# Four attention steps' weighted sums in one visit, and VectorE's other work put where it falls due

## The chip, the core and the metric

The kernel runs on one core of a Trainium2 chip. A core has five engines with their own instruction streams: TensorE multiplies matrices and writes PSUM, VectorE and ScalarE work on SBUF and PSUM, GpSimd on SBUF, and SyncE here issues every DMA. Streams run each in its own order and meet at semaphores only. PSUM has eight banks of 128 x 512 float32. The metric is the device time of one execution in microseconds (us).

## What is computed

A layer of attention and MLP, then a layer norm, then a feed-forward block with a choice of one of eight low-rank experts per token, then a layer norm. There are 4 batches of 2048 tokens of width 256, 16 heads of width 16. Only every eighth token attends to all tokens (the others attend to themselves), so a batch has 256 queries.

```python
xn = _ln(x, ln1_g, ln1_b)
q, k, v = split(xn @ w_in.T + b_in)
allowed = (idx % 8 == 0)[:, None] | (idx[:, None] == idx[None, :])
attn = softmax(where(allowed, q k / sqrt(16), -inf))
x1 = x + (attn v) @ w_out.T + b_out
x2 = x1 + gelu(_ln(x1, ln2_g, ln2_b) @ w1.T + b1) @ w2.T + b2
y = layernorm(x + x2)
base = y @ wi_W.T + wi_b
for i in range(8):
    inter = relu(base + (y @ lora_A[i].T) @ lora_B[i].T)
    out += (argmax(y @ gate_W.T + gate_b) == i) * (inter @ wo_W.T + wo_b)
result = layernorm(y + out)
```

## The kernel before

A function, `build_steps`, writes one list of named steps, and every engine walks through this list and issues its own part of each step. So the list sets each engine's order; what a step waits for is a semaphore count that is worked out from the list.

The MLP work is cut into blocks of 512 tokens, M for the first MLP and F for the expert one, and a block into eight items `i` of 128 hidden columns. An item has the steps `up` (two halves: 3 and 3 products of 512 columns, with one more in an F block), `ev` (ScalarE casts the activated item, GpSimd subtracts the cast to get the low part) and `dn` (two halves by tokens, 6 products of 256 columns each). Each float32 factor is split into a high and a low part, so a product is three (`three`, lines 1567 to 1569). `dn` of an item stands two items behind its `up` (`LAG = 2`). When a block's last `dn` has been issued, `sum` adds it to the rows (VectorE, line 1525), `la` takes statistics (lines 1316 to 1330), then `lb` or, for F, `lf` on GpSimd normalises, `st` stores.

To begin a block, `tn` (two parts) turns its rows through the array: four transposes on TensorE (1791), a copy on ScalarE (1179), a subtraction for the low part on VectorE (1512). For an F block `ga` makes the gate logits (16 products, 1803; ScalarE copies them, 1191), `pick` chooses the expert in four parts of three small VectorE operations (1356 to 1373), `pi` turns the choice (1809).

Attention of a batch is 64 steps `s`: head pair `p = s // 8`, key block `kk = s % 8`. A step has `sc` (scores: four products with 50 rows, two head halves side by side, line 1745; ScalarE's exponential into a buffer `prob`, 1172), `mx` (the row maxima of a later pair, 12 steps ahead: two products with 48 rows, 1730; VectorE reduces them, 1442), and `at` (weighted sums: products with 32 columns, line 1756). The last eight maxima of a pair give `ng` (1449 to 1457) and `mt` (a small turn, 1735, that a DMA sends to the scores' operand). After a pair's last step `or` copies the sums out (1466), `ot` turns them (1762), `os` normalises them (1477 to 1482). All `mx` of the attention stages use PSUM banks 2 and 3, `sc` banks 0 and 1, `at` bank 4; `up`, `tn`, `ga`, `pi`, `mt` and `ot` share bank 5, `dn` has 6 and 7. A step that takes a bank waits until its last user's result has been read.

In a stage of attention these steps stand between the MLP items: each item is four quarters (`up` first half, `up` second half, `dn` first half, `dn` second half with `ev`), and 64 steps are spread over the quarters of 16 items (batches 0 and 3) or 24 items (batches 1 and 2). At every even step the two earlier steps' weighted sums come first:

```python
if s % 2 == 0:
    weighted(s - 2)
    weighted(s - 1)
scores(s)
maxima(s)
turns(s)
moves(s)
```

There are two `prob` buffers. `tn`, `ga` and `pi` of the next block hang on the third quarter of set items, `mt` and `ot` (from `turns`) wait in a list and are put in where none of these stands, in the third or last quarter.

Of the kernel before, what the change touches and what calls it, by code (L numbers as in the profile page):

```python
# [44 lines left out]
LEAD = MPP + MPP // 2  # L45
EARLY = LEAD
# [34 lines left out]
def build_steps():  # L81
# [5 lines left out]
    def down(half):  # L87

        if len(pending) <= LAG:
            return  # L90
        i = pending[0]
        put(("dn", i, half))
        if half == 1:
            pending.pop(0)
            if i % FT == FT - 1:
                put(("sum", i // FT))

    def drain():
        while pending:
            i = pending.pop(0)  # L100
            put(("dn", i, 0))
            put(("dn", i, 1))
            if i % FT == FT - 1:
                put(("sum", i // FT))
# [155 lines left out]
    def attention(b):  # L260
# [16 lines left out]
        alone, late = [], []  # L277
# [8 lines left out]
        def turned_out(s, taken):  # L286

            if alone and (alone[0][0][0] == "mt" or len(blocks) == 2 or s % KK in (0, 7) or not taken):
                for one in alone.pop(0):
                    put(one)  # L290
                    if one[0] == "ot":
                        late.append(("os", *one[1:]))
# [3 lines left out]
        def moves(s):  # L296
            p, kk = s // KK, s % KK
            if kk == 1 and p and p + 2 < PAIRS:
                put(("kld", b, p + 2))
            if s == 4:  # L300
# [10 lines left out]
        def step(s):  # L311

            if s % 2 == 0:
                weighted(s - 2)
                weighted(s - 1)
            scores(s)
            maxima(s)
            turns(s)
            moves(s)

            while late:
                put(late.pop(0))

        s, hook = 1, []

        places = [(0, 2, 4, 7)] * 2 if len(blocks) == 2 else [(0, 2, 3, 7), (0, 1, 3, 7), (1, 2, 4, 7)]
        for quarter in range(4 * n):

            ahead = min(2, quarter // 2) if len(blocks) == 2 else 0
            while s < STEPS_B and s * 4 * n <= (quarter + ahead) * STEPS_B:  # L330
                step(s)
                s += 1
            i, part = FT * blocks[0] + quarter // 4, quarter % 4
            k, f = i // FT, i % FT
            ready = k + 1
            at = places[k - blocks[0]]
            if part == 0:
                put(("up", i, 0))
            elif part == 1:
                put(("up", i, 1))  # L340
                pending.append(i)
                after(k - 1, f, 4)
                rows_in(k, f, 6)
                if f == at[2] + 1:
                    put(("pick", ready, 1))
                if f == at[2] + 2:
                    put(("pick", ready, 3))
            elif part == 2:
                down(0)
                hook = dict(zip(at, ([("tn", ready, 0)], [("tn", ready, 1), ("xw", ready)], [("ga", ready)], [("pi", ready)]))).get(f, [])  # L350
                taken = bool(hook)
                if hook and hook[0][0] == "pi" and alone and alone[0][0][0] == "mt":
                    turned_out(s, False)
                for one in hook:
                    put(one)
                if not hook:
                    taken = turned_out(s, False)
            else:
                put(("ev", i))
                turned_out(s, taken)  # L360
                down(1)
                if f == at[2]:
                    put(("pick", ready, 0))
                if f == at[2] + 1:
                    put(("pick", ready, 2))
        assert s == STEPS_B and not alone and not late
# [3 lines left out]
    def tail(b):  # L370
# [32 lines left out]
        while pending:  # L403
            i = pending.pop(0)
            put(("dn", i, 0))
            put(("dn", i, 1))
# [37 lines left out]
def N(*step):  # L444
    return COUNT[step]

# [41 lines left out]
for _s in STEPS:  # L488
# [26 lines left out]
    elif _w == "dn" and _s[1] % FT == 0:  # L515
# [86 lines left out]
def attention_ffn_kernel(nc, x, w_in, b_in, w_out, b_out, w1, b1, w2, b2, ln1_g, ln1_b, ln2_g, ln2_b,  # L602
                         gate_W, gate_b, wi_W, wi_b, wo_W, wo_b, lora_A, lora_B, out):
    ctx = ExitStack()
    with ctx:
# [74 lines left out]
        prob = [place(f"prob{i}", [P, 2, 2, QW], F32, m0 + 4096 * i)[0] for i in range(2)]  # L680
# [12 lines left out]
        x1g, _ = place("x1g", [P, NQ, D], F32, r1 + 5120)  # L693

# [99 lines left out]
        def _(sp):  # L794
# [25 lines left out]
            def step(what, *a):  # L820
# [75 lines left out]
                elif what == "ldg":  # L896
                    sp.wait_ge(stq, 48 * KT * N("pq", b))
# [71 lines left out]
        def _(pool):  # L969
# [10 lines left out]
            def step(what, *a):  # L980
# [6 lines left out]
                elif what == "xc":  # L987
                    c = a[1]
                    n = N("xc", b, c)
                    x_c = xin[PLACE[c] % XB]  # L990
                    if n > 4:
# [872 lines left out]
```

## Time and profile before

| | |
|---|---|
| median of 3 runs | 1442.04 us (1440.31 to 1442.88) |
| the profiled execution's span, first to last instruction | 1437.3 us |
| TensorE busy in the span | 1386.3 us (96%), 10103 products |
| VectorE, ScalarE, GpSimd busy | 854.4, 734.6, 647.8 us |
| granted TensorE clock, mean | 0.995 |
| attention stages in the span, about | 159 to 312, 480 to 655, 823.5 to 998, 1167 to 1320 us |

The profile is of one execution; for it only its span is known, which lies 4.7 us under the median of the timed runs. A product is shown with the time from its start to its modelled end, while the next one starts earlier; so the busy share overstates, and the distances from start to start tell the pace. In brackets stands the idle time of the engine before an instruction and what released it.

### The profile page before, as it was taken

Reading aid. Unit: us, or ns where it says so; the run is one execution under the profiler, and the core shown is the slowest. Engines: PE = TensorE matmul, PEld = TensorE weight load, DVE = VectorE, ACT = ScalarE, POOL = GpSimd, SP = SyncE. Lnnn points to the kernel's source line nnn. Section 1 sums busy time; section 2 is a strip of 40 time slices with the busy share of each in tenths; the row PEclk is TensorE's granted clock in tenths of the full one; section 3 lists DMA queues with packets and bytes.
Section 4 is the critical chain, followed back from the end, with each engine's and each line's share of the span. In section 5 each row is a group of like instructions: output and inputs, shape, how many; then the busy total and the mean of one; then the engine's idle time right before and its main releaser. Section 6 shows DMA issues by size and latency. Waiting matters only on the chain.

```text
span 1437.3 us, 26412 instructions
## 1 busy us (share of the span) xinstructions
PE 1386.3 (96%) x10103; PEld 1066.3 (74%) x10103; DVE 854.4 (59%) x1823; ACT 734.6 (51%) x1103; POOL 647.8 (45%) x533
## 2 busy tenths in 40 slices
PE   6799999999999999999999999999999999999997
PEld 5688665678888766668888866667888876556996
DVE  6748576636656666555647576763675657762332
ACT  3444555553544555564444555555444455655442
POOL 3554321328754414145865432333776442132755
PEclk9899999999999999999999999999999999999999
DMA  7565223215561132212682213220556212310100
GB/s 246 161 181 107 57 45 67 55 38 192 190 164 47 50 68 51 56 45 84 210 214 62 74 38 75 57 53 20 189 189 158 74 45 44 80 26 23 52 16 30
DMA packets 91394, 130.51 MB, mean 91 GB/s; under 512 B 8314, under 2 KB 68180, under 8 KB 88148
## 3 DMA queue, kind: packets, MB, share of 16 engines
q1 hardware_dynamic: 91268, 128.82, 32.9%
q8 instruction: 81, 1.33, 0.4%
q14 instruction: 45, 0.37, 0.1%
HBM read 68.08 MB, written 60.57 MB: 90 GB/s over the span
## 4 chain that ended last, share of the span: by engine, by line
PE 79%; DVE 10%; POOL 4%; issue 2%; ACT 2%; DMA 0%; SPq 0%; POOLq 0%; DVEq 0%; ACTq 0%
PE ps L1567 19%; PE ps L1568 16%; PE ps L1569 16%; PE ps L1756 8%; PE ps L1745 7%; PE ps L1730 4%; DVE mx L1442 3%; PE ps L1803 2%; PE ps L1791 2%; PE ps L1825 2%; DVE stats L1316 2%; POOL rows L1042 1%; ACT prob L1172 1%; PE ps L1688 1%; PE ps L1762 1%
## 5 line engine op out<-in xcount | busy, mean ns | idle before, releaser
L1442 DVE TENSOR_REDUCE mx<-ps 128x2 f32<-128x1024 f32 x256 | 311.1, 1223 | 179.0 <-PE ps L1730 176.9
L1172 ACT ACTIVATE prob<-ps 128x1024 f32<-128x1024 f32 x256 | 262.6, 1026 | 180.4 <-PE ps L1745 180.2
L1057 POOL TENSOR_TENSOR hid1l<-gel,hid1h 128x512 fp32r<-128x512 f32 x85 | 111.2, 1309 | 202.2 <-ACT hid1h L1214 202.1
L1057 POOL TENSOR_TENSOR hid2l<-gel,hid2h 128x512 fp32r<-128x512 f32 x85 | 111.1, 1307 | 197.6 <-ACT hid2h L1214 197.5
L1057 POOL TENSOR_TENSOR hid0l<-gel,hid0h 128x512 fp32r<-128x512 f32 x86 | 112.4, 1307 | 191.6 <-ACT hid0h L1214 191.5
L1206 ACT ACTIVATE gel<-ps,cols 128x512 f32<-128x512 f32 x128 | 88.2, 689 | 180.7 <-PE ps L1569 169.5
L1745 PEld LDWEIGHTS ps<-qslot,kslot 50*128 50x128 f32 x1024 | 76.2, 184 | 91.0 <-issue 65.8
L1208 ACT ACTIVATE gel<-ps 128x512 f32<-128x512 f32 x128 | 76.6, 598 | 120.9 <-PE ps L1825 119.7
L1756 PE MATMUL ps<-prob,vals 128*32 128x256 f32 x2048 | 137.5, 385 | 0.2
L1745 PE MATMUL ps<-qslot,kslot 50*128 50x256 f32 x1024 | 128.9, 330 | 4.2 <-ACT prob L1172 4.1
L1730 PE MATMUL ps<-kslot,qslot 48*128 48x512 f32 x512 | 105.8, 424 | 4.8 <-DVE mx L1442 4.4
L1756 PEld LDWEIGHTS ps<-prob,vals 128*32 128x32 f32 x2048 | 53.2, 109 | 54.9 <-ACT prob L1172 14.8
L1036 POOL TENSOR_TENSOR rstd<-vare,mhalf 128x4 f32<-128x4 f32 x47 | 48.3, 1028 | 76.6 <-DVE vare L1330 74.9
L1042 POOL TENSOR_SCALAR rows<-rows,mv,rstd 128x256 f32<-128x256 f32 x60 | 73.5, 1234 | 0.0
L1567 PE MATMUL ps<-turned0h,wih 128*128 128x512 f32 x128 | 58.8, 459 | 0.0
L1730 PEld LDWEIGHTS ps<-kslot,qslot 48*128 48x128 f32 x512 | 46.3, 184 | 16.5 <-DVE mx L1442 8.8
L1567 PE MATMUL ps<-turned1h,wih 128*128 128x512 f32 x128 | 57.2, 447 | 0.0
L1214 ACT ACTIVATE hid0h<-gel 128x512 fp32r<-128x512 f32 x86 | 54.0, 628 | 1.3
L1567 PE MATMUL ps<-turned1h,w1h 128*128 128x512 f32 x128 | 54.3, 424 | 0.1
L1512 DVE TENSOR_TENSOR turned1l<-ps,turned1h 128x512 fp32r<-128x512 f32 x32 | 22.1, 690 | 54.3 <-ACT turned1h L1179 54.2
L1214 ACT ACTIVATE hid2h<-gel 128x512 fp32r<-128x512 f32 x85 | 53.5, 629 | 1.3
L1214 ACT ACTIVATE hid1h<-gel 128x512 fp32r<-128x512 f32 x85 | 53.4, 628 | 1.3
(245 smaller groups left out, 3943.9 us busy)
## 6 DMA issues: line engine op xcount, KB each, us to landing
k_d<-kst SPq DMA_DIRECT2D x192, 128.0 KB
kslot<-k_d SPq DMA_DIRECT2D x64, 384.0 KB
xin<-in_L_attn_x SPq DMA_DIRECT2D x32, 256.0 KB, 4.3
rows<-xs_d SPq DMA_DIRECT2D x16, 512.0 KB, 6.3
y_d<-rows SPq DMA_DIRECT2D x15, 512.0 KB, 3.1
rows<-y_d SPq DMA_DIRECT2D x15, 512.0 KB, 4.5
out<-rows SPq DMA_DIRECT2D x15, 512.0 KB, 3.2
xs_d<-xin SPq DMA_DIRECT2D x28, 256.0 KB, 2.7
```

The source lines that it names most:

```text
L1042: nc.gpsimd.tensor_scalar(y[:, i, :], y[:, i, :], mv[:, k % 2, i, 0:1], rstd[:, k % 2, i:i + 1], ALU.subtract, ALU.mult).then_inc(final_do ...
L1057: nc.gpsimd.tensor_tensor(hid[i % RING][1][:], gel[i % 2][:], hid[i % RING][0][:], ALU.subtract).then_inc(lo_done, 1)
L1172: nc.scalar.activation(prob[(n - 1) % 2][:].rearrange("p e i q -> p (e i q)"), ps[:, 0:2, :].rearrange("p a n -> p (a n)"), ACT.Exp).then_ ...
L1206: nc.scalar.activation(gel[i % 2][:], ps[:, UP, :], ACT.Gelu, bias=cols[:, B1C + f:B1C + f + 1]).then_inc(act_done, 1)
L1214: nc.scalar.activation(hid[i % RING][0][:], gel[i % 2][:], ACT.Copy).then_inc(hi_done, 1)
L1442: nc.vector.tensor_reduce(best[:, :, j % NQ], ps[:, at:at + 2, :], AX.X, ALU.max).then_inc(maxr_done, 1)
L1567: mm(o, l[0], r[0], start=start, stop=False, skip_group_check=True)
L1568: mm(o, l[0], r[1], start=False, stop=False, skip_group_check=True)
L1569: return mm(o, l[1], r[0], start=False, stop=stop, skip_group_check=True)
L1730: last = mm(ps[:, bank + e, :], qslot[p % SLOTS][half, P * t:P * t + P], kslot[p % SLOTS][half, 512 * piece:512 * piece + 512], start=True ...
L1745: last = mm(ps[:, e, QW * i:QW * i + QW], kslot[p % SLOTS][half, at:at + P], qslot[p % SLOTS][half, :], start=True, stop=True)
L1756: last = mm(ps[at:at + PR, OUT, 0:QW], vals[:, v:v + PR], prob[(n - 1) % 2][:, e, i, :], start=kk == 0, stop=kk == KK - 1)
```

## The change

A visit takes one step, and every fourth visit two: the scores and maxima of step s, then the weighted sums of four steps (s - 3 to s), then scores and maxima of s + 1. A stage is cut into three parts an item (16 items) or four (24 items, a visit at every second part), so that 48 visits lie evenly. `prob` has four buffers; the two new ones lie over `xg` and `x1o`, which is why the residual load `ldg` moves to the last step and some waits are added. `dn` is issued in four parts instead of two, `sum` in two halves, each with its half of the statistics (`ls`) behind it, and `la` right after. The four `pick` parts stand right behind `ga`. Only `os` is kept back, to the visit behind.

```diff
+GROUP = 4
...
+        def job(cost, *what):
+            if what[0][0] == "os":
+                jobs.append((cost, unit[0], what))
+            else:
+                for one in what:
+                    put(one)
...
+        def visit(s):
+
+            unit[0] += 1
+            taken = [s]
             scores(s)
             maxima(s)
-            turns(s)
-            moves(s)
...
+            if s % GROUP == GROUP - 1 or s == STEPS_B - 2:
+                slot(1.25)
+                for one in range(s + 1 - GROUP, s + 1) if s % GROUP == GROUP - 1 else (s - 2, s - 1):
+                    weighted(one)
+                scores(s + 1)
+                maxima(s + 1)
+                taken.append(s + 1)
+            for one in taken:
+                turns(one)
+                moves(one)
+            slot(small)
+            return taken[-1] + 1
+
+        def down_part(i, h, j):
+            put(("dn", i, h, j))
+            if i % FT == FT - 1 and j == 1:
+                blk = i // FT
+                job(0.7, ("sum", blk, h))
+                job(0.8, ("ls", blk, 2 * h), ("ls", blk, 2 * h + 1))
+                if h == 1:
+                    job(0.8, ("la", blk))
...
+        parts = 3 if len(blocks) == 2 else 4
...
+            if s < STEPS_B and (parts == 3 or at_part % 2 == 0):
+                s = visit(s)
...
+                if hook and hook[0][0] == "ga":
+                    for what in range(4):
+                        job((1.4, 0.6, 0.8, 0.6)[what], ("pick", ready, what))
...
-        prob = [place(f"prob{i}", [P, 2, 2, QW], F32, m0 + 4096 * i)[0] for i in range(2)]
...
+        prob = [place(f"prob{i}", [P, 2, 2, QW], F32, at)[0] for i, at in enumerate((m0, m0 + 4096, r1 + 3072, r1 + 8192))]
```

TensorE in the first items of batch 0's attention, before. `qslot` by `kslot` are scores, `kslot` by `qslot` maxima, `prob` by `vals` weighted sums, `ust` the end of an `up`.

```order
L1825 MATMUL ps<-ust,bst 128x512
L1756 MATMUL ps<-prob_107,vals 32x256 x4
L1756 MATMUL ps<-prob_108,vals 32x256 x4
L1745 MATMUL ps<-qslot_115,kslot_112 128x256 x4
L1730 MATMUL ps<-kslot_113,qslot_116 128x512 x2
```

The same place now:

```order
L1921 MATMUL ps<-ust,bst 128x512
L1841 MATMUL ps<-qslot_113,kslot_110 128x256 x4
L1826 MATMUL ps<-kslot_111,qslot_114 128x512 x2
L1852 MATMUL ps<-prob_120,vals 32x256 x4
L1852 MATMUL ps<-prob_121,vals 32x256 x4
L1852 MATMUL ps<-prob_122,vals 32x256 x4
L1852 MATMUL ps<-prob_123,vals 32x256 x4
L1841 MATMUL ps<-qslot_113,kslot_110 128x256 x4
L1826 MATMUL ps<-kslot_112,qslot_115 128x512 x2
```

Sums of four steps now stand in one row, between two pairs of scores and maxima.

TensorE a few products later in the same item, before. `ident,rows` are the four transposes of `tn`, `ident,negs` is the small turn `mt`.

```order
L1569 MATMUL ps<-w2h,hid1l 128x256
L1791 MATMUL ps<-ident,rows_97 128x128 x4
L1756 MATMUL ps<-prob_107,vals 32x256 x4
L1756 MATMUL ps<-prob_108,vals 32x256 x4
L1745 MATMUL ps<-qslot_115,kslot_112 128x256 x4
L1730 MATMUL ps<-kslot_114,qslot_117 128x512 x2
L1735 MATMUL ps<-ident,negs 8x128
L1567 MATMUL ps<-w2h,hid1h 128x256
```

The same place now:

```order
L1665 MATMUL ps<-w2h,hid1l 128x256
L1887 MATMUL ps<-ident,rows_97 128x128 x4
L1831 MATMUL ps<-ident,negs 8x128
L1663 MATMUL ps<-w2h,hid1h 128x256
L1664 MATMUL ps<-w2l,hid1h 128x256
```

The small turn follows the transposes at once; a visit stood between.

VectorE behind the second gate of batch 0's attention stage, before. `mx<-ps` are the maxima's reductions, `uall`, `pickm` and `picke` the choice.

```order
L1356 TENSOR_TENSOR uall<-gcopy 128x160
L1357 TENSOR_TENSOR uall<-uall,gateb 128x4x8
L1358 TENSOR_REDUCE pickm<-uall 128x4
L1442 TENSOR_REDUCE mx<-ps 128x2 x2
L1360 TENSOR_TENSOR picke<-uall,pickm 128x32
L1361 TENSOR_TENSOR picke<-picke,rank 128x32
L1362 TENSOR_REDUCE pickm<-picke 128x4
L1466 COPY oraw<-ps 128x256
L1442 TENSOR_REDUCE mx<-ps 128x2 x2
```

The same place now, from the second operation of the choice:

```order
L1449 TENSOR_TENSOR uall<-uall,gateb 128x4x8
L1450 TENSOR_REDUCE pickm<-uall 128x4
L1452 TENSOR_TENSOR picke<-uall,pickm 128x32
L1453 TENSOR_TENSOR picke<-picke,rank 128x32
L1454 TENSOR_REDUCE pickm<-picke 128x4
L1456 TENSOR_TENSOR picke<-picke,pickm 128x32
L1458 TENSOR_TENSOR uall<-uall,picke 128x4x32
L1461 CAST us<-uall 128x4x32
L1463 TENSOR_TENSOR us<-uall,us 128x4x32
L1464 COPY us<-us 128x4x32
L1465 MEMSET us 128x4x2
L1534 TENSOR_REDUCE mx<-ps 128x2 x3
```

All twelve operations of a choice now stand between two reductions.

## Rows read from the trace of the kernel before

**Rows 1.** The profile page's head: span and instructions.

```profile
span 1437.3 us, 26412 instructions
```

**Rows 2.** By stage: us, busy of TensorE, its loads, VectorE, ScalarE, GpSimd; clock.

```profile
159.00:312.00 153.00, 148.56 (x1265) 91.87 (x1264) 95.11 (x175) 92.24 (x122) 36.65 (x29) 1.00 0.23 51
480.00:655.00 175.00, 172.78 (x1445) 116.23 (x1444) 105.32 (x200) 103.75 (x142) 54.96 (x43) 1.00 0.22 52
```

**Rows 3.** Timeline (start, length, engine, line), TensorE: a visit without sums.

```profile
823.26 0.28 PE L1569 MATMUL ps<-w2h,hid0l 128*128 128x256 f32 x1
823.47 0.51 PE L1745 MATMUL ps<-qslot,kslot 50*128 50x256 f32 x4
823.81 0.40 PE L1730 MATMUL ps<-kslot,qslot 48*128 48x512 f32 x2
...
824.37 0.28 PE L1568 MATMUL ps<-w2l,hid0h 128*128 128x256 f32 x1
```

**Rows 4.** Timeline, TensorE: a visit with two steps' sums.

```profile
844.22 0.28 PE L1569 MATMUL ps<-wfh,hid0l 128*128 128x256 f32 x1
844.43 1.07 PE L1756 MATMUL ps<-prob,vals 128*32 128x256 f32 x16
845.43 0.51 PE L1745 MATMUL ps<-qslot,kslot 50*128 50x256 f32 x4
...
846.44 0.40 PE L1568 MATMUL ps<-turned0l,wih 128*128 128x512 f32 x1
```

**Rows 5.** Timeline, TensorE: sums straight behind maxima.

```profile
171.21 0.50 PE L1730 MATMUL ps<-kslot,qslot 48*128 48x512 f32 x2
171.64 1.39 PE L1756 MATMUL ps<-prob,vals 128*32 128x256 f32 x16
```

**Rows 6.** Costliest groups: busy, mean ns, idle before and releaser; the maxima.

```profile
L1730 PE MATMUL ps<-kslot,qslot 48*128 48x512 f32 x512 | 105.8, 424 | 4.8 <-DVE mx L1442 4.4
```

**Rows 7.** Timeline, TensorE: scores that wait for an exponential.

```profile
1305.70 0.50 PE L1745 MATMUL ps<-qslot,kslot 50*128 50x256 f32 x4
1307.32 0.50 PE L1745 MATMUL ps<-qslot,kslot 50*128 50x256 f32 x4 [0.23 <-ACT prob L1172]
```

**Rows 8.** Timeline, all engines: maxima that wait for a reduction.

```profile
559.71 1.23 DVE L1442 TENSOR_REDUCE mx<-ps 128x2 f32<-128x1024 f32 x1
...
560.99 0.50 PE L1730 MATMUL ps<-kslot,qslot 48*128 48x512 f32 x2 [0.22 <-DVE mx L1442]
...
561.53 1.23 DVE L1442 TENSOR_REDUCE mx<-ps 128x2 f32<-128x1024 f32 x1 [0.60 <-PE ps L1730]
```

**Rows 9.** Timeline, VectorE: operations of a choice.

```profile
570.06 1.25 DVE L1357 TENSOR_TENSOR uall<-uall,gateb 128x32 f32<-128x32 f32 x1
...
644.82 0.18 DVE L1364 TENSOR_TENSOR picke<-picke,pickm 128x32 f32<-128x32 f32 x1
...
645.96 0.23 DVE L1372 COPY us<-us 128x128 f32<-128x128 f32 x1
```

**Rows 10.** Timeline, VectorE: sum and statistics of a finished block.

```profile
554.72 1.27 DVE L1525 TENSOR_TENSOR rows<-rows,ps 128x512 f32<-128x512 f32 x2
...
557.78 1.40 DVE L1316 BATCH_NORM_STATS2 stats<-rows 128x6 f32<-128x256 f32 x4
```

**Rows 11.** Timeline, all engines: transposes, their low part, the small turn.

```profile
188.32 0.60 PE L1791 MATMUL ps<-ident,rows 128*128 128x128 f32 x4
...
189.65 0.68 DVE L1512 TENSOR_TENSOR turned0l<-ps,turned0h 128x512 fp32r<-128x512 f32 x1
...
190.39 0.28 PE L1735 MATMUL ps<-ident,negs 128*8 128x128 f32 x1
```

**Rows 12.** Timeline, TensorE: a turn behind gate products, transposes behind a turn.

```profile
815.10 0.27 PE L1735 MATMUL ps<-ident,negs 128*8 128x128 f32 x1 [0.53 <-ACT gcopy L1191]
...
537.72 0.64 PE L1809 MATMUL ps<-ident,us 128*98 128x128 f32 x4 [0.36 <-ACT mT L1153]
```

**Rows 13.** Timeline, ScalarE: the first exponential of a stage.

```profile
824.91 1.02 ACT L1172 ACTIVATE prob<-ps 128x1024 f32<-128x1024 f32 x1
```

More of the change, by code:

```diff
@@ L91, in down @@
         i = pending[0]
-        put(("dn", i, half))
+        for j in range(2):
+            put(("dn", i, half, j))
         if half == 1:
@@ L95, in down @@
             if i % FT == FT - 1:
[L96 to L104, printed above, removed]
+                for h in range(2):
+                    put(("sum", i // FT, h))
     def piece(b, q, part):
@@ L275, in weighted, with slot, flush @@
                     put(("or", b, s // KK))
-        alone, late = [], []
+        alone, jobs, unit = [], [], [0]
+        def job(cost, *what):
[4 more added lines that the diff above has]
+                    put(one)
+        def slot(room):
+            spent = 0.0
+            while jobs and jobs[0][1] < unit[0] and (not spent or spent + jobs[0][0] <= room):
+                cost, _, what = jobs.pop(0)
+                spent += cost
+                for one in what:
+                    put(one)
+        def flush(*kinds):
+            while any(one[0] in kinds for _, _, what in jobs for one in what):
+                for one in jobs.pop(0)[2]:
+                    put(one)
         def turns(s):
@@ L286, in turned_out @@
         def turned_out(s, taken):
-            if alone and (alone[0][0][0] == "mt" or len(blocks) == 2 or s % KK in (0, 7) or not taken):
+            if alone and (alone[0][0][0] == "mt" or len(blocks) == 2 or s % KK in (0, 5, 6, 7) or not taken):
+                if alone[0][0][0] == "ot":
+                    flush("os")
                 for one in alone.pop(0):
@@ L309, in moves @@
                         put(one)
[L311 to L315, printed above, removed]
+        small = 0.5 if len(blocks) == 2 else 1.0
+        def visit(s):
+            unit[0] += 1
+            taken = [s]
             scores(s)
             maxima(s)
-            turns(s)
-            moves(s)
-            while late:
-                put(late.pop(0))
-        s, hook = 1, []
-        places = [(0, 2, 4, 7)] * 2 if len(blocks) == 2 else [(0, 2, 3, 7), (0, 1, 3, 7), (1, 2, 4, 7)]
@@ L327, in attention @@
[L327 to L333, printed above, removed]
+            if s % GROUP == GROUP - 1 or s == STEPS_B - 2:
[5 more added lines that the diff above has]
+                taken.append(s + 1)
@@ new lines, in ended @@
+        def ended(k, f):
+            if k < 0:
+                return
+            what = BLOCKS[k][0]
+            if what == "M" and f == 4:
+                flush("la")
+                put(("lb", k))
+            if what == "F" and f in (3, 4):
+                flush("la")
+                put(("lf", k, f - 3))
+            if f == 5:
+                put(("st", k))
+        s = 1
+        places = [(0, 2, 4, 7)] * 2 if len(blocks) == 2 else [(0, 2, 3, 7), (0, 1, 3, 7), (1, 2, 4, 7)]
+        parts = 3 if len(blocks) == 2 else 4
@@ L334, in attention @@
+        owed = None
+        for at_part in range(parts * n):
+            if s < STEPS_B and (parts == 3 or at_part % 2 == 0):
+                s = visit(s)
+            i, part = FT * blocks[0] + at_part // parts, at_part % parts
             k, f = i // FT, i % FT
@@ L404, in tail @@
             i = pending.pop(0)
-            put(("dn", i, 0))
-            put(("dn", i, 1))
+            for h in range(2):
+                for j in range(2):
+                    put(("dn", i, h, j))
         for h in range(2):
@@ L1314, in ln_a @@
                 j = k % 2
[L1315 removed]
+                for i in range(CT if ("ls", LN_STEPS[k][1], 0) not in COUNT or LN_STEPS[k][0] != "la" else 0):
                     nc.vector.bn_stats(stats[:, j, i, :], y[:, i, :]).then_inc(stat_done, 1)
```

114 lines of the change are left out of this document (74 added, 40 removed).

## The prediction, made before the changed kernel ran

> **What bounds the kernel now.** I read the span first, then the busy time by stage, then TensorE's starts inside one stage. The span is 1437.3 us [rows 1]; the median of the three timed runs, 1442.04, is 4.7 above it, so I add a change of the span to the median. Only the four attention stages change their order. Two are short (batches 0 and 3: two MLP blocks of eight items beside 64 steps), two are long (batches 1 and 2: three blocks). One of each is shown: TensorE is busy 148.6 of 153 us and 172.8 of 175 at a granted clock of 1.00, its 2.4 GHz level, VectorE 95 and 105, ScalarE 92 and 104 [rows 2]. So TensorE's order sets the time, and another engine counts only where TensorE stands and waits for it. Busy hides part of such waits, since a product is shown for 0.28 to 0.5 us while the next can start after 0.11 to 0.23. I therefore go by starts.
>
> **What an attention visit costs.** A visit with scores and maxima alone: last down product 823.26, second one after the visit 824.37, 1.11 us; two down products at their free pace of 0.12 taken off leave 0.87 [rows 3]. A visit with two steps' weighted sums ahead: 844.22 to 846.44, 2.22, less one down (0.12) and one up product (0.23), leaves 1.87; from the first sum's product to the scores it is 1.00 for 16 products, that is 0.216 for each four, and the rest is the turn between the array's tilings [rows 4]. From maxima to weighted sums there are only two cases, 0.43 from start to start [rows 5], of which 0.21 is the maxima's own work.
>
> **What the change saves.** Four steps were two visits of each kind, 2 x 0.87 + 2 x 1.87 = 5.48. Now they are two single visits and one group: entry 0.21, scores to maxima 0.34, maxima to sums 0.43, eight rounds of four 1.87 to the next scores, 0.34, then 0.65 until the second product behind; 3.84 less 0.35 for two ordinary products is 3.48. With the singles 5.22: 0.26 saved for each visit that goes. The order has 62 to 64 visits in a stage before and 48 now, so 14 and 16 go: 2 x (14 + 16) x 0.26 = **-15.7 us**.
>
> Second, TensorE's waits of before go or move. Its idle before maxima products, mostly for VectorE's reduction, is 4.8 us in all [rows 6]; with the hidden part, and with those before scores and before small transposes, taken as every start in these stages that is over 0.04 us later than is usual for its pair, I find 10 us in a short stage and 4 in a long one: **-28 us** at most, if all go. The exponentials' part does go: in the group three sums stand ahead of the one that needs the newest exponential, and the single visits lie 1.8 us apart or more, where scores that wait for an exponential start 1.62 after the scores ahead [rows 7].
>
> **What the change adds.** All maxima of these stages share one pair of PSUM banks. A reduction ends, the next maxima product follows 0.05 later (559.71 + 1.23, 560.99), and its reduction starts 0.54 after it [rows 8], which I take as 0.45 where the product had not waited. So two maxima products need some 1.72 us. In a short stage the single visits now follow one another 1.9 and 1.8 us apart, in a long one 2.3 and 2.5, and 2.63 lie between a group's two. Whatever VectorE does between two reductions beyond the gap that these leave (0.6 to 0.7, 1.1 to 1.3, 1.4) delays the later one, and TensorE stands at the maxima after that.
>
> Gate choice. The twelve small operations of a gate stood in four quarters, several reductions apart; now all stand between two reductions. Free, the last six take 1.4 us from 644.82 on, the first six as much. An operation that meets GpSimd's subtraction takes 1.25 (570.06), where those six average under 0.25 [rows 9], and ScalarE's copy that releases that subtraction now follows the gate's copy at once, so I take one meeting: 4.0 us, bounds 2.9 and 5. In a long stage, from a maxima product as zero: six down products to 1.14, sixteen gate products to 2.73, the gate's copy done 0.8 later, choice from 3.55 to 7.55, the next reduction from there to 8.8. The maxima product behind it would have started at 6.5: 2.3 us of waiting. In a short stage, 3.3. Two gates of a long stage and one of a short one have maxima behind them: 4 x 2.3 + 2 x 3.3 = **+15.8**.
>
> Here the page named SBUF — State Buffer of the Trainium skill (Who interferes with whom) bears: an operation of VectorE with two SBUF inputs and a GpSimd instruction that reads SBUF take turns whole, by who starts first. The 1.25 us agree. By it the meeting costs at most one subtraction, and the sum is the above; had the two engines shared without waiting, it would be 6 us less.
>
> Block ends. Sum and statistics of a finished block, 1.27 us and, from 557.78 to the reduction at 559.71, 1.93 [rows 8, 10], were one visit or more apart; now half of them follow the first down half, the other half the second, with one reduction at most between. In a long stage nothing is between: 3.4 us where 1.1 are free and the next maxima have 0.8 to spare, 1.45; with a turned block's low part (0.68) in the same place twice, 1.7 and 1.85. In a short stage 0.5 + 1.3, and with the output normalisation in it 2.3. 2 x (5.0 + 4.1) = **+18.2**.
>
> The shared bank. Transposes, gate products and up products use one PSUM bank. Before, a turned block's transposes and the small turn of the maxima had a visit between; in the short stages the two now stand back to back, four times in each. The turn must wait until ScalarE has copied and VectorE has subtracted: transposes from 188.32 on, the last at 188.65, subtraction 189.65 to 190.33, turn at 190.39 [rows 11]. That is 1.7 after the last transpose, where 0.11 is the free pace: 8 x 1.6 = **+12.7**. A turn right behind gate products idles 0.53, and four transposes right behind a turn 0.36 [rows 12]; 0.17 more is hidden in each. New are two of the first kind without maxima behind (0.7) and ten of the second, the turned output behind the turn (0.5): **+6.6**.
>
> The start. The first scores now have the second ones 1.56 us behind them in each stage. The first exponential starts at 824.91 for scores at 823.47 and takes 1.02 [rows 3, 13], so the second scores wait 0.96: 4 x 0.96 = **+3.8**. Product starts after a wait lose about 0.1 more, some 24 times, and small things (copies ahead of exponentials, the last visits without maxima) 0.4 to 1 a stage: **+4**.
>
> At nothing I cost: the down step cut in halves (same products, one wait less), the key loads a step earlier (they wait for the same scores as before), two more buffers for the exponentials, and the residual load put at the stage's end. That load, two GpSimd additions of 1.3 us and the subtraction behind them come before the down products of that item, which stand two items later; if that cover failed it would cost up to 3 us a batch.
>
> **Sum.** -15.7 - 28 + 15.8 + 18.2 + 12.7 + 6.6 + 3.8 + 4 = **+17.4 us**: span 1454.7, median **1459**. Bounds of the unknown: choice without the meeting -6, with two +6; halves of the block end better hidden -5; the output normalisation meeting the subtraction in short stages (1.7 instead of 0.76) up to +10; the turn from maxima to sums, from two cases, -3 to +3. Together some 1448 to 1472.
>
> **Rivals.** *VectorE keeps pace* (faster): the merged visits bring 15.7 and the old waits 28, and the bursts land where TensorE has other work. It decides at the maxima product two visits after a burst: if that starts on time, picks, block ends and most bank waits are not paid, and between 20 and 40 us of new waits are left: 1442 - 44 + 20 = 1418, up to 1438. For it speaks that VectorE is busy only 60% of the stages; against it, that one bank pair serves all maxima. Chance 0.18. *A wash*: a quarter to a third of the added terms is hidden, 1438 to 1445, chance 0.12. *The bursts pile up* (slower than I say): a late reduction pushes the next burst into the next gap, and the projection behind starts with a delayed GpSimd: 1473 to 1485, chance 0.08. *The order does not do what is said*: the instruction order shows four steps' sums between two scores, so I give it nothing.
>
> [...]
>
> **How the numbers follow.** Forecast, 1446 to 1472: 0.62. A comparison of this kernel can tell about 0.2%, 2.9 us. Faster by more takes the first rival and a little of the wash: 0.2; the same: 0.1; slower: 0.7. The range leaves out the quicker half of the first rival and the piled-up case: 1430 to 1473.
>
> **What would show it.** Right: maxima products idle for VectorE's reduction by 25 us or more in all (4.8 now); idle before the small turn and the turned output for ScalarE and VectorE, over 10 us; stages of about 156 and 181 us. Wrong: long stages under 172 us, choice bursts after which the next maxima start on time, or a projection that changes by over 1 us.

## The result: 36 us slower, twice the forecast

The changed kernel takes 1476.85 us (median of six, 1476.07 to 1483.98), the kernel before 1441.17: 35.7 us more, a ratio of 1.026 (95% interval 1.0244 to 1.0280). Forecast were 17.4 us more, 1459, and a range up to 1473. The direction was right and the size was not. Where one execution of a version lay far above its others (6478 us in e10_turns_apart, 1551 in e7_long_waits), it is left out of that version's median below.

The profiled execution is the slowest of the six. The head of its page, and its row for the maxima (that of before is in [rows 6]):

```profile
span 1482.2 us, 26416 instructions
L1826 PE MATMUL ps<-kslot,qslot 48*128 48x512 f32 x512 | 105.8, 424 | 34.7 <-DVE mx L1534 32.3
```

The idle time before maxima has gone from 4.8 to 34.7 us. By stage (the columns of [rows 2]: us, busy of TensorE, its loads, VectorE, ScalarE, GpSimd, granted clock, DMA), the four attention stages, and the first projection between them:

```profile
163.00:327.00 164.00, 146.51 (x1264) 94.71 (x1263) 97.12 (x175) 92.24 (x122) 34.95 (x27) 0.97 0.21 48
327.00:496.00 169.00, 167.20 (x1067) 146.14 (x1059) 104.58 (x239) 75.32 (x128) 108.40 (x90) 1.00 0.46 134
496.00:678.00 182.00, 170.73 (x1444) 120.24 (x1443) 106.41 (x200) 102.73 (x142) 54.30 (x42) 0.98 0.22 50
847.30:1029.40 182.10, 170.84 (x1445) 120.44 (x1443) 106.39 (x200) 102.84 (x142) 54.26 (x42) 0.98 0.21 50
1198.30:1364.60 166.30, 148.72 (x1260) 95.32 (x1259) 93.63 (x162) 91.77 (x121) 33.44 (x25) 0.95 0.20 42
```

From first scores to last sums the stages were 152.6, 174.7, 174.7 and 152.5 us; they are 164.0, 181.9, 182.0 and 166.3: 39.9 more in all. The long ones are 1 us above the forecast (181), the short ones 8 to 10 above it (156). The projection is the same to 1 us. Another 4 us of this execution lie ahead of the first stage, in code that the change leaves alone; the other executions have spans of 1474 to 1476.

The column to look at is the last but two: the granted clock was 1.00 in every attention stage before, and it is 0.95 to 0.98 now.

**One burst, close up.** First VectorE and TensorE together in the second stage (start, length, engine, line): the gate choice, the maxima behind it, the products behind those.

```profile
526.81 0.33 DVE L1448 TENSOR_TENSOR uall<-gcopy 128x160 f32<-128x160 f32 x1 [1.86 <-ACT gcopy L1283]
...
527.35 0.39 PE L1826 MATMUL ps<-kslot,qslot 48*128 48x512 f32 x2
...
527.62 1.11 DVE L1452 TENSOR_TENSOR picke<-uall,pickm 128x32 f32<-128x32 f32 x1
527.68 1.93 PE L1852 MATMUL ps<-prob,vals 128*32 128x256 f32 x32
...
529.54 0.50 PE L1841 MATMUL ps<-qslot,kslot 50*128 50x256 f32 x4
...
530.64 0.07 DVE L1465 MEMSET us<- 128x8 f32 x1
530.74 1.23 DVE L1534 TENSOR_REDUCE mx<-ps 128x2 f32<-128x1024 f32 x1
...
532.02 0.57 PE L1826 MATMUL ps<-kslot,qslot 48*128 48x512 f32 x2 [1.98 <-DVE mx L1534]
...
532.53 0.79 PE L1663 MATMUL ps<-turned0h,wih 128*128 128x512 f32 x1
...
533.12 0.63 PE L1664 MATMUL ps<-turned0l,wih 128*128 128x512 f32 x1
533.55 0.63 PE L1665 MATMUL ps<-turned0h,wil 128*128 128x512 f32 x1
```

The maxima of 527.35 are done before 527.8, but their reduction has to wait behind the whole choice (526.81 to 530.71, with one operation that met GpSimd, 1.11 us) and starts at 530.74. The next maxima, ready behind the scores of 529.54, start at 532.02. That much was foretold: a choice of 4.0 us and a wait of 2.3. What was not: the up products behind the wait start 0.59 and 0.43 apart, where 0.34 and 0.23 are usual. The same place by stretches:

```profile
529.00:532.30 3.30, 1.32 (x18) 0.61 (x10) 2.96 (x10) 1.02 (x1) 0.00 (x0) 1.00 0.00 0
532.30:535.70 3.40, 3.40 (x9) 2.15 (x7) 2.76 (x7) 0.00 (x0) 0.00 (x0) 0.50 0.00 0
535.70:539.00 3.30, 2.94 (x24) 2.19 (x23) 1.23 (x1) 2.59 (x5) 0.56 (x1) 1.00 0.02 5
```

TensorE stood for most of the first stretch; in the second it is busy throughout at a granted clock of 0.50, its 1.2 GHz level, while its products start further apart; in the third the clock is back. Eleven such places lie in the four stages (one is twice as long, and the expectation of e1_all_due counts it as two), none in those of before. By the stage rows the loss is at most 164.0 x 0.03 + 182 x 0.02 x 2 + 166.3 x 0.05 = 20.5 us. Taking every product that starts in one of these stretches and how much later it comes than is usual behind its neighbour, I find **17.8 us**. I call this the clock's loss below, and give it for each kernel's profiled execution.

What TensorE waited for in the stages (us in total, times, longest):

```profile
PE ps L1826 <- DVE mx L1534: 32.3, 26, 2.3
PE ps L1831 <- DVE turned1l L1604: 5.7, 4, 1.4
PE ps L1831 <- DVE turned0l L1604: 5.7, 4, 1.4
PE ps L1831 <- ACT gcopy L1283: 3.7, 7, 0.5
PE ps L1858 <- ACT mT L1237: 3.6, 10, 0.4
PE ps L1841 <- ACT prob L1264: 3.6, 4, 0.9
```

These are the waits of the prediction, but for 8 of the 26 before maxima (the copy, taken apart below) and two more small turns behind gate products than it had. The largest part of what was missing looked like the clock. That, and the terms themselves, is what the experiments test.

### The profile page after: what moved, and what is told of

It reads as the page before. It is cut to its first block, busy times and chain, and to the rows that moved or that the text cites. A ratio compares the mean times of both kernels' runs of the same rounds, so it can differ in the third digit from the quotient of the medians.

```text
span 1482.2 us, 26416 instructions
## 1 busy us (share of the span) xinstructions
PE 1385.8 (93%) x10103; PEld 1084.2 (73%) x10103; DVE 863.6 (58%) x1823; ACT 732.4 (49%) x1103; POOL 647.8 (44%) x533
## 4 chain that ended last, share of the span: by engine, by line
PE 75%; DVE 12%; POOL 4%; issue 3%; ACT 2%; DMA 0%; SPq 0%; POOLq 0%; DVEq 0%; ACTq 0%
PE ps L1663 18%; PE ps L1664 15%; PE ps L1665 15%; PE ps L1852 8%; PE ps L1841 6%; PE ps L1826 4%; DVE mx L1534 3%; PE ps L1899 2%; PE ps L1921 2%; PE ps L1887 2%; POOL rows L1126 1%; DVE stats L1408 1%; ACT prob L1264 1%; DVE rows L1616 1%; PE ps L1858 1%
## 5 line engine op out<-in xcount | busy, mean ns | idle before, releaser
L1826 PE MATMUL ps<-kslot,qslot 48*128 48x512 f32 x512 | 105.8, 424 | 34.7 <-DVE mx L1534 32.3
L1852 PE MATMUL ps<-prob,vals 128*32 128x256 f32 x2048 | 130.5, 396 | 0.0
L1852 PEld LDWEIGHTS ps<-prob,vals 128*32 128x32 f32 x2048 | 61.1, 113 | 51.7 <-issue 18.9
L1558 DVE COPY oraw<-ps 128x256 f32<-128x256 f32 x32 | 13.6, 425 | 80.2 <-PE ps L1852 50.8
L1137 POOL TENSOR_TENSOR rows<-rows,wob 128x1024 f32<-128x1024 f32 x16 | 38.1, 2380 | 43.0 <-PE ps L1887 43.0
L1663 PE MATMUL ps<-wfh,hid0h 128*128 128x256 f32 x176 | 55.6, 316 | 0.0
```

The costliest lines, as they stand in the source:

```text
L1663: mm(o, l[0], r[0], start=start, stop=False, skip_group_check=True)
L1826: last = mm(ps[:, bank + e, :], qslot[p % SLOTS][half, P * t:P * t + P], kslot[p % SLOTS][half, 512 * piece:512 * piece + 512], start=True ...
L1852: last = mm(ps[at:at + PR, OUT, 0:QW], vals[:, v:v + PR], prob[prob_of(p, kk)][:, e, i, :], start=kk == 0, stop=kk == KK - 1)
```

## The experiments

Line numbers differ a little between the versions; the names in the rows are the same. For each kernel:

| version | us | ratio to before (95%) | idle before maxima | clock's loss |
|---|---|---|---|---|
| changed kernel | 1476.85 | 1.026 (1.0244 to 1.0280) | 34.7 | 17.8 |
| e4_fill | 1466.84 | 1.019 (1.0178 to 1.0208) | 16.7 | 4.6 |
| e2_pick_due | 1457.49 | 1.013 (1.0112 to 1.0142) | 22.0 | 11.8 |
| e3_ends_due | 1460.39 | 1.014 (1.0129 to 1.0159) | 18.2 | 14.3 |
| e1_all_due | 1439.20 | 1.0005 (0.999 to 1.002) | 7.9 | 0 |
| e5_turn_first | 1468.51 | 1.020 (1.0175 to 1.0222) | 23.7 | 22.3 |
| e10_turns_apart | 1468.31 | 1.021 (1.0179 to 1.0247) | 36.4 | 25.9 |
| e6_due_and_apart | 1434.18 | 0.996 (0.9944 to 0.9977) | 1.4 | 10.6 |
| e9_all_apart | 1427.55 | 0.9915 (0.9901 to 0.9929) | 8.5 | 0 |
| e11_sum_at_once | 1419.00 | 0.985 (0.9839 to 0.9864) | 9.3 | 1.6 |
| e12_copy_later | 1410.44 | 0.979 (0.9774 to 0.9811) | 1.8 | 0 |
| e7_long_waits (kernel before, delayed) | 1480.51 | 1.029 (1.0269 to 1.0320) | 32.3 | 13.9 |
| e8_short_waits (kernel before, delayed) | 1480.18 | 1.028 (1.0264 to 1.0299) | 29.3 | 3.1 |

**Is it the clock?** Some 220 products whose results nobody reads go into 22 of the long waits; they write an unused half of a PSUM bank.

```diff
+FILL = {(b, m // MPP, m % MPP): n for b in range(B) for m, n in
+        (((23, 6), (34, 14), (55, 12)) if b in (0, LAST) else ((19, 7), (24, 13), (40, 9), (46, 14)))}
...
+if what == "mx":
...
+    fill(FILL.get(a, 0))
+elif what == "mt" and seen[1] == "tn":
+    fill(9)
```

> The changed kernel with extra products, whose results nobody reads, put on TensorE into 22 of its long waits (the 14 longest ones before maxima, 6 to 14 products each, and the 8 before the small turn behind transposes, 9 each); nothing else moves, every wait ends when it did. Theory A: the granted clock stays at 1.00 in the stages and the time falls although work was added, by up to the 17.8 us that the half-clock stretches hold: 1463 us (1459 to 1468). Theory C (the low clock is a mark of idle time and costs nothing; the 18 us that the prediction lacks are waits): 1475 us or more.

1466.84 us: 10 us faster with more work. The place shown above, here in TensorE's timeline (L1776 is the filler):

```profile
522.92 0.50 PE L1861 MATMUL ps<-qslot,kslot 50*128 50x256 f32 x4
523.26 1.70 PE L1776 MATMUL ps<-kslot,qslot 48*128 48x256 f32 x13
525.37 0.50 PE L1846 MATMUL ps<-kslot,qslot 48*128 48x512 f32 x2 [0.41 <-DVE mx L1534]
525.80 0.50 PE L1663 MATMUL ps<-turned0h,wih 128*128 128x512 f32 x1
526.14 0.39 PE L1664 MATMUL ps<-turned0l,wih 128*128 128x512 f32 x1
526.37 0.39 PE L1665 MATMUL ps<-turned0h,wil 128*128 128x512 f32 x1
```

The maxima start 2.45 us after the scores (525.37 less 522.92); without filler it was 2.48. The wait is as long as ever, yet the up products behind it are 0.34 and 0.23 apart again. The stages by the same view:

```profile
160.70:320.10 159.40, 150.77 (x1332) 101.02 (x1331) 97.09 (x175) 92.14 (x122) 35.11 (x27) 1.00 0.22 49
489.30:669.80 180.50, 174.41 (x1488) 124.56 (x1486) 106.33 (x200) 102.83 (x142) 54.02 (x42) 0.99 0.22 51
838.60:1017.50 178.90, 172.79 (x1487) 123.21 (x1486) 106.34 (x200) 102.78 (x142) 54.22 (x42) 1.00 0.22 51
1186.50:1348.80 162.30, 153.61 (x1329) 101.88 (x1327) 93.57 (x162) 91.89 (x121) 32.35 (x25) 0.98 0.20 43
```

The clock's loss falls by 13.2 us (17.8 to 4.6), the four stages of the profiled executions by 13.3 (694.4 to 681.1), the median of all executions by 10. In all 22 places TensorE still idles 0.15 to 0.58 us between the last filler product and the one that waits, so no wait got longer. Theory C, that low clock is a mark and not a cost, is out.

**Long waits or idle time as such?** Two kernels without anything of the change, only the kernel before with reductions repeated in the long stages: three reductions five times, or 24 twice. The first as an edit (the second does it once more, at every second index from 14 to 60):

```diff
+for again in range(4 if b in (1, 2) and MPP * p + j in (28, 40, 52) else 0):
+    nc.vector.tensor_reduce(best[:, :, j % NQ], ps[:, at:at + 2, :], AX.X, ALU.max).then_inc(again_done, 1)
...
```

> The kernel before, with nothing of the change: in each long stage three reductions are done five times instead of once, so that the next maxima wait some 4.3 us, six times in all, 26 us of waits. Theory A (each wait this long is followed by a stretch at half clock that costs 1.7 us or more): 26 + 10, so 1476 us (1471 to 1482), six stretches. Theory C (a wait costs its length): 1466 (1462 to 1469), whatever the clock reads.

> The kernel before, with 24 reductions of each long stage done twice: by the spacing of the maxima there, waits of 0 to 0.8 us, 21 us in all, none long. Theory A: no stretch at half clock, 1461 us (1456 to 1467), the waits alone. If it is the sum of idle time and not the single long wait after which the clock falls, stretches at half clock show here too and the time is 1470 or more.

The long waits: 1480.51 us (three executions, 1480.24 to 1485.06), inside the range of theory A; six waits of 4.4 to 5.5 from start to start, and a stretch at half clock behind each of the six. By starts, the long stages got 27.7 us more of waits and 13.9 of clock's loss. One of the six, its maxima and the two stretches on both sides of it:

```profile
532.91 0.80 PE L1735 MATMUL ps<-kslot,qslot 48*128 48x512 f32 x2 [4.59 <-DVE mx L1447]
...
528.00:532.00 4.00, 0.32 (x4) 0.11 (x2) 3.90 (x4) 1.43 (x2) 0.00 (x0) 0.97 0.63 109
532.00:538.50 6.50, 5.59 (x32) 3.27 (x32) 2.08 (x2) 0.44 (x2) 0.00 (x0) 0.50 0.00 0
```

The short waits missed their expectation: 1480.18 against 1461. The extra reductions met VectorE's other work oftener than the spacing of the maxima had told, and the waits came to 33.7 us, not 21. For the clock the run is clear all the same. More waiting, by 48 repeated reductions and mostly in short pieces, has a clock's loss of only 3.1: two stretches, each right behind one of the few long waits (2.45 and 1.73 us late; two others, of 2.10 and 1.76, had none). Here the long waits cost half of themselves again (13.9 of 27.7), the time in small pieces a tenth (3.1 of 33.7). That the waits of the maxima alone, without groups of four steps, bring the clock down is shown too.

**The bursts.** The changed kernel has a waiting list from which VectorE's work could come out piece by piece at later visits, but lets only the output normalisation into it. These three let in more:

```diff
-if what[0][0] == "os":
+if what[0][0] in ("os", "pick", "sum", "ls", "la"):
```

> The changed kernel, but VectorE's gate choice (four parts) and the sum and statistics of a finished block stand in the waiting list and come out one by one at later visits, where the changed kernel puts them down at once; TensorE's order stays. Theory A (bunched work of VectorE makes the maxima wait, and each wait of some 2 us is followed by a stretch at half clock): TensorE's idle before maxima falls from 32 us to about 10, the transposes' 8 waits of 1.7 stay, stretches at half clock go from 12 to 4 or fewer, time 1443 us (1435 to 1452). Theory B (the merged visits leave too little room between the maxima, whoever stands between them): waits of 25 us or more stay and the time is above 1465.

> The changed kernel with only the gate choice handed out over later visits; block ends stay bunched. By the prediction's term the choices cost 15.8 us of waits; with their share of the half-clock stretches (theory A) 22 to 25, so 1453 us (1447 to 1462). If the choices are harmless, 1474 or more.

 (here only "pick" is added)

> The changed kernel with only sum and statistics of finished blocks handed out over later visits; choices stay bunched. By the prediction's term block ends cost 18.2 us; with the half-clock stretches behind them about 23, so 1454 us (1448 to 1464). If they are harmless, 1474 or more.

 (here "sum", "ls" and "la")

1439.2, 1457.5 and 1460.4 us. With choice and block ends handed out, the 36 us are gone: TensorE's order of the changed kernel, VectorE's work spread, and the time is that of before. The choices alone bring 19.4 (6.0 of it the clock's loss, by the profiled executions), the block ends alone 16.5 (3.5). The maxima's row in the first of them, and its long stage:

```profile
L1826 PE MATMUL ps<-kslot,qslot 48*128 48x512 f32 x512 | 102.5, 410 | 7.9 <-DVE mx L1534 7.5
...
479.70:651.60 171.90, 167.15 (x1445) 117.84 (x1443) 102.19 (x200) 102.83 (x142) 53.99 (x42) 1.00 0.23 53
```

Theory B, that merged visits leave too little room whoever stands between them, falls. The ten executions of this version spread from 1433.8 to 1443.8, those above 1441.5 all at a mean granted clock of 0.989, the 1433.8 at 0.995; the profiled one is the fastest. What decides it in a given execution stays open.

**The shared bank.** In the short stages the small turn is put ahead of the transposes and gate products, between two down products:

```diff
 down_part(one, 0, 0)
+if hook and hook[0][0] in ("tn", "ga") and parts == 3 and alone and alone[0][0][0] == "mt":
+    turned_out(s, False)
 down_part(one, 0, 1)
```

> The changed kernel, but in the short stages the small turn of the maxima stands between the two down products that come ahead of a block's transposes or gate products, instead of right behind these; VectorE's work stays bunched. By the prediction's term the 8 turns behind transposes cost 1.58 us each and the 4 behind gate products 0.7: 15 us of waits go. Some of it is given back, since the maxima that wait for VectorE then come earlier; with a third given back and two or three half-clock stretches gone, 1463 us (1457 to 1469). If the maxima's waits take it all back, 1472 or more.

1468.5, the upper end of what was expected, but not by the way that was expected. With the small turn gone from behind the transposes and gate products, the output's turn, next in the same list, stood there: of the 15.4 us of waits in these places 12.3 stayed under another name. What went is in front of the short stages' maxima, which were 22.1 us late in all and are 9.8: mostly a wait of VectorE's copy, 8.7 us, that is gone because the output's turn now comes early (its rows follow below). The output's turn behind the transposes, in a short stage of e6_due_and_apart:

```profile
265.09 0.66 PE L1892 MATMUL ps<-ident,rows 128*128 128x128 f32 x4
...
267.17 0.44 PE L1863 MATMUL ps<-ident,oraw 128*128 128x128 f32 x2 [1.41 <-DVE turned1l L1609]
```

That is the wait of 1.69 from the last transpose, with another name on it. The output's turn was then barred from that place as well:

```diff
-turned_out(s, taken)
+if parts == 4 or not (hook and hook[0][0] in ("tn", "ga")):
+    turned_out(s, taken)
```

> The changed kernel with the small turn and the output's turn kept away from transposes and gate products in the short stages, VectorE's work still bunched. The waits of the prediction's term on the shared bank go in full now (the first try left 6 of 1.69 and 4 of 0.81 behind the output's turn): 1468.5 less 12, with up to half given back in waits for VectorE: 1460 us (1455 to 1465). If they are all given back, 1467 or more.

1468.3 us in the median of three, 1466.2 to 1479.8 (the profiled one): nothing beyond the first try, the arm that the expectation put at "1467 or more". The waits behind transposes and gate products are gone, 12.3 us, and 13.6 came back in front of the short stages' maxima (9.8 to 23.4). Of these 8.7 are the copy again: VectorE's copy of a finished pair's sums waits for the output's turn of the pair before, and a reduction stands behind it. With the output's turn early (first row, e5_turn_first) the copy waits only for its own sums, with the turn late (second row, this version) for the turn:

```profile
218.21 0.42 DVE L1560 COPY oraw<-ps 128x256 f32<-128x256 f32 x1 [0.67 <-PE ps L1854]
...
225.35 0.42 DVE L1561 COPY oraw<-ps 128x256 f32<-128x256 f32 x1 [3.47 <-PE ps L1861]
```

The rest are longer waits behind choices and block ends; one that was 2.47 us from start to start in the changed kernel is 3.20. Against the changed kernel, which has the copy's wait too, the larger part of the term is there. The short stages, the only ones that these edits touch, are 158.9 and 158.5 us long where they were 164.0 and 166.3: 12.9 less, with 15.4 of waits at the turns and 3.4 of the clock's loss gone, and against that 1.4 more before the maxima and some 4 in small waits (the transposes, which now follow the small turn, start some 0.18 later each time). The profiled execution hides this, since its long stages, in the changed kernel's order, took 185.9 and 189.3 us for 182.0 and 182.1. Their maxima were late by the same amounts (8.6 and 9.0 us for 8.6 and 8.6), but the clock's loss there was about 17 us instead of 6. A short and a long stage:

```profile
160.60:319.50 158.90, 147.04 (x1264) 95.11 (x1263) 96.68 (x175) 91.18 (x122) 35.07 (x27) 0.97 0.22 49
488.75:674.60 185.85, 174.66 (x1440) 123.00 (x1443) 106.27 (x200) 103.01 (x142) 53.99 (x42) 0.95 0.21 49
```

So the clock's loss of one execution is not set by the order alone, and differences of some 10 us in that column can be the execution's.

**Both together.** The handed-out work of the first version with the turns apart, and three down products (the expectation says six) between the small turn and the output's turn in the long stages:

> All of VectorE's side work handed out over later visits, the small turn ahead of transposes and gate products in the short stages, and six down products between the small turn and the output's turn in the long ones. If the terms add up: 1439.2 less 15 (turns of the short stages) less 5 (output turns), 1420 us, range 1415 to 1430, no stretch at half clock in the stages, faster than before by 0.7 to 1.7%. If VectorE is the limit in the short stages, 1433 or more.

1434.2, faster than before by 0.4%, but not 1420: the output's turn stood behind transposes and gate products here too (row above), and behind five of these ten places the clock fell, 10.6 us: two after 1.69 from start to start, three after 0.81. With that barred:

> As the version with the work handed out and the turns apart, but the output's turn, too, no longer stands behind transposes or gate products in the short stages (in that version it had slipped into the place that the small turn left: 6 waits of 1.69 and 4 of 0.81 from start to start). 12 us of waits go; if the half-clock stretches of that version (7 in the profiled execution, 10.6 us) hang on them, 8 to 10 more: 1418 us (1412 to 1426). If the clock falls whatever stands there, 1424 to 1430; if VectorE takes the gain back in the maxima, 1430 or more.

1427.6, no stretch at half clock in the stages. That is above the 1418 forecast and within the arm "if the clock falls whatever stands there" in its number, though not in its reason: the clock did not fall, and 7 us came back in front of the short stages' maxima (idle 1.4 to 8.5). Again it is the copy, which had no such wait while the output's turn came early: eight maxima are 1.09 to 1.12 us late behind it.

**Two orders of VectorE.** In the long stages the next block's first down products waited 1.2 to 1.5 us for the handed-out sum. The list then holds "os", "pick", "ls" and "la" only:

> As the version with everything apart, but a finished block's sum (two halves of 0.63 us) is done at once, only statistics and choice are handed out. The first down products of the next block wait for that sum in the long stages (1.2 and 1.5 us more than usual, once or twice in each): 3 to 5 us less than the version with everything apart, if the halves fit between two reductions; 0 to 4 us more if they make maxima wait instead.

1419.0, 8.5 us less, more than expected; the long stages are 3.2 us shorter each (171.1 to 167.9), and 3.4 of the difference between the two profiled executions lie ahead of the first stage, where nothing differs. What remained before the maxima is mostly the copy's wait, one that no step of the prediction has. It is in the changed kernel already, here in a short stage:

```profile
226.96 0.40 PE L1826 MATMUL ps<-kslot,qslot 48*128 48x512 f32 x2
...
228.10 0.38 PE L1858 MATMUL ps<-ident,oraw 128*128 128x128 f32 x2
...
230.20 0.50 PE L1826 MATMUL ps<-kslot,qslot 48*128 48x512 f32 x2 [0.93 <-DVE mx L1534]
...
228.59 0.42 DVE L1558 COPY oraw<-ps 128x256 f32<-128x256 f32 x1 [2.78 <-PE ps L1858]
228.93 1.22 DVE L1534 TENSOR_REDUCE mx<-ps 128x2 f32<-128x1024 f32 x1
```

The maxima of 226.96 are ready before 227.4. Their reduction stands behind VectorE's copy of a finished pair's sums, and that copy waits for the output's turn of the pair before (228.10), because both use one buffer. VectorE idles with work at hand, and the next maxima are 1.09 us late, four times in each short stage: 8.7 us. Last, the copy goes behind that reduction:

```diff
-if s % KK == KK - 1:
+if s % KK == KK - 1 and not later:
     put(("or", b, s // KK))
...
 scores(s + 1)
 maxima(s + 1)
+if len(blocks) == 2 and s % KK == KK - 1:
+    put(("or", b, s // KK))
```

> As the version with the sums at once (1419.0 us), but in the short stages VectorE's copy of a finished head pair's weighted sums stands behind the reduction of the group's second maxima instead of ahead of it. In the trace that copy waits for the output's turn of the pair before, and the reduction, whose maxima are done, waits behind it: four maxima in each short stage are 1.1 us late. If that order is the cause, 8.7 us of TensorE's idle before maxima go to under 1 and the time is 1411 us (1407 to 1415); if the reduction is late for another reason, 1417 to 1421.

1410.44, as expected, 2.1% faster than before. The maxima's row:

```profile
L1833 PE MATMUL ps<-kslot,qslot 48*128 48x512 f32 x512 | 101.9, 408 | 1.8 <-DVE mx L1541 1.7
```

## Why the prediction was right in its waits and wrong in its size

Point by point, in us over the four stages of the profiled execution, by TensorE's starts:

| step of the prediction | forecast | measured |
|---|---|---|
| merged visits, and the old waits that go | -15.7 - 28 = -43.7 | -42.3 (what remains) |
| gate choice and block ends, before maxima | 15.8 + 18.2 = 34.0 | 30.6 |
| the copy ahead of a reduction | none | 8.7 |
| turn behind transposes | 12.7 | 12.6 |
| turn behind gate products, output's turn behind the turn | 6.6 | 8.8 |
| second scores of a stage | 3.8 | 3.8 |
| clock and small things | 4 | 17.8 |
| sum | 17.4 | 40.0 |

The maxima came 28.7 us later than before in all, where 10.6 of old lateness went: 39.3, of which 8 x 1.09 are the copy. The bank terms are 8 x (1.69 - 0.11), 4 x (0.81 - 0.11) and 10 x (0.63 - 0.03), the start 4 x 0.96. The first row was not measured by itself: it is what remains of 39.9 once the others are taken off, so small things are in it. In e1_all_due, whose profiled execution lost nothing to the clock, the same sum leaves some -40. One part of it I can name: sums straight behind maxima start 0.32 to 0.36 after them as a rule (527.35 to 527.68 above), not the 0.43 that I had from two cases, which helps each of the groups by some 0.1.

**The step that failed** is the last term: "Product starts after a wait lose about 0.1 more, some 24 times". The waits it foretold were there (26 for reductions, though 8 of these are the copy's, next point). What lies behind them was priced from waits of before, which are short, and the granted clock of 1.00 was read as given. At eleven places the clock fell, and the term measures 17.8. All 8 waits of 2.1 us or more from start to start had a stretch at half clock, of the 14 between 1.4 and 1.75 two had one, and one stretch stood behind 0.81. The filler shows that the clock, and not the idle time, holds most of that; the long and short waits in the kernel before show that it needs nothing else of the change. By the medians the sum is 35.7. The profiled execution is 7.1 us above its median; some 4 of that lie ahead of the first stage, where it had a stretch at 0.91 (80 to 120 us).

The Trainium skill has the pattern, in TensorE: Matmul & The Clock Gate, A second HAM failure mode: psum-queue depth-cycling: pauses between groups of products that cycle through PSUM banks let the clock go to and fro between its levels, and throughput suffers though the typical product looks as fast as ever. The trace agrees in that the waits listed with the result are for PSUM banks, the maxima's mean of 424 ns is that of [rows 6], and 17.8 us are gone. It does not agree where the section puts this down to pauses that come often: the many short ones of e8_short_waits lost 3.1 us, the six long ones of e7_long_waits 13.9.

**Second**, the copy ahead of the reduction was not in the sum. I had listed what VectorE does between two reductions, but not that an entry of its row can wait for TensorE while a reduction behind it is ready. The copy's wait also explains what the versions gave back: it is in the changed kernel, absent in e5_turn_first and e6_due_and_apart, back in e10_turns_apart and e9_all_apart, and e12_copy_later takes it out by itself, 8.6 us.

**Third**, a term that is taken away can bring up another wait. The waits behind transposes and gate products were priced rightly and can be won for the larger part (the short stages of e10_turns_apart), but each place that the small turn left was taken by the next turn in the list, and each time the output's turn moved, the copy's wait came or went with it. With the bursts gone the edits on the turns brought 11.6 us (e1_all_due to e9_all_apart), of 20 forecast.

**The rivals.** That VectorE keeps pace fell as the burst above shows; what spoke for it, a VectorE busy only 60%, is what made the spread version possible. The bursts piling up had the right time (1473 to 1485) for another reason: the long stages took 181.9 us where 181 were forecast, some 3 of them the clock's loss, so nothing piled up. What would show the forecast right was there: idle for the reduction 32.3 (25 or more), idle before the turns 18.7 (over 10), projections unchanged. By those marks the mechanism holds; they could not show the clock, since I had not asked for it.

## What to carry to other kernels

Price a wait of TensorE as its length plus what the clock does behind it, and look in the trace for stretches at the lower level. Here 30 of 35 waits of 2.1 us or more had one, shorter ones now and then. Work of another engine that stands in its row ahead of something TensorE needs belongs in small pieces, one to a gap, and never behind an entry that can itself wait. After moving a step out of a bad place, look at what stands there now.

## What the chip showed that was not expected

Products added to a waiting TensorE made the kernel 10 us faster (1476.85 to 1466.84). Six waits of 4.4 to 5.5 us cost 13.9 us beyond themselves; 33.7 us in mostly short pieces cost 3.1. The length of a wait does not decide alone. In the profiled executions of all versions and of the kernel before, a stretch at half clock stood at 30 of 35 waits of 2.1 us or more from start to start, at 14 of 82 between 1.4 and 1.9, at none of some 195 others from 0.6 to 1.4, yet at 11 of 28 waits of 0.81 behind sixteen gate products. The same waits had stretches in one execution and none in another (e6_due_and_apart and e1_all_due, the long stages of e10_turns_apart and of the changed kernel); what else decides was not tried.
